# Cross attention over 16 batches: another beginning, input copies in four parts, value sums in pairs of steps, values in three pieces

## The reference

```python
x = x + xattn(layernorm(x), ctx_1024, ctx_1024, Wq, bq, Wk, bk, Wv, bv, Wo, bo)
x = x + attn_ref(layernorm(x), ...)     # Mamba block and MLP
x = x + ffn_ref(layernorm(x), ...)      # 8 experts, 2 chosen per token

def xattn(query, key, value, ...):      # D 128, 16 heads of 8, batches 16, queries 64, keys 1601
    q = split_heads(query @ Wq.T + bq)
    k = split_heads(key @ Wk.T + bk)
    v = split_heads(value @ Wv.T + bv)
    scores = einsum('bhqd,bhkd->bhqk', q, k) / sqrt(8)
    weights = softmax(scores, axis=-1)
    out = einsum('bhqk,bhkd->bhqd', weights, v)
    return out.transpose(0, 2, 1, 3).reshape(b, -1, 128) @ Wo.T + bo
```

## Time and profile before

| what | us |
|---|---|
| median of 3 runs (range) | 650.39 (646.67 to 653.92) |
| the profiled execution | 646.16 |
| its span in the trace | 644.3 |
| start to the first scores of batch 0 | 67.6 |
| the 16 rounds of attention | 67.6 to 422 |
| Mamba, MLP and experts | 422 to 644.3 |

### The profile page before, as it was taken

One profiled execution on the slowest core, in us unless ns is written; L12 is line 12 of the kernel. 1 busy time (PEld: TensorE's weight loads), 2 busy tenths in 40 slices (PEclk: granted clock), 3 DMA queues, 4 the chain that ended last, 5 costly groups with the idle time before them and its releaser, 6 DMA issues. The chain is left out here.

```text
span 644.3 us, 17592 instructions
## 1 busy us (share of the span) xinstructions
PE 544.0 (84%) x7470; PEld 356.4 (55%) x7470; DVE 442.6 (69%) x755; ACT 353.7 (55%) x641; POOL 254.6 (40%) x138
## 2 busy tenths in 40 slices
PE   2666899898897898999999989855677888999997
PEld 1232555554564554555565556542356566777776
DVE  5365878776785776888788878069887575454544
ACT  4641477666675576677677768932742423333331
POOL 3184676646645654657566310078045000000000
PEclk9985799998998999999999999995858779999999
DMA  5736764753753835844763250023002000000001
GB/s 178 113 99 99 100 155 87 131 69 65 132 67 65 133 43 90 131 59 93 114 80 57 39 68 4 3 68 88 1 5 107 1 1 2 1 0 0 1 0 34
DMA packets 16117, 41.56 MB, mean 65 GB/s; under 512 B 3190, under 2 KB 6014, under 8 KB 15930
## 3 DMA queue, kind: packets, MB, share of 16 engines
q1 hardware_dynamic: 15324, 40.09, 34.8%
q10 hardware_dynamic: 720, 0.41, 0.2%
HBM read 19.70 MB, written 0.52 MB: 31 GB/s over the span
## 5 line engine op out<-in xcount | busy, mean ns | idle before, releaser
L603 DVE TENSOR_REDUCE half_max<-wide 128x2 f32<-128x802 f32 x256 | 243.6, 989 | 69.1 <-PE wide L376 64.7
L527 ACT ACTIVATE probs<-score 128x512 f32<-128x512 f32 (+1 forms) x416 | 225.5, 594 | 64.6 <-PE score L396 64.2
L413 PE MATMUL sums<-probs,values 128*32 128x192 f32 (+3 forms) x3328 | 135.9, 282 | 9.7 <-issue 8.0
L413 PEld LDWEIGHTS sums<-probs,values 128*32 128x32 f32 (+1 forms) x3328 | 88.2, 110 | 66.9 <-issue 33.2
L376 PE MATMUL wide<-k_stack,q_cur 48*128 48x401 bf16 x512 | 91.3, 354 | 8.5 <-DVE half_max L603 4.0
L396 PE MATMUL score<-q_cur,k_stack 50*128 50x128 bf16 (+1 forms) x1664 | 85.1, 222 | 13.0 <-issue 5.5
L396 PEld LDWEIGHTS score<-q_cur,k_stack 50*128 50x128 bf16 (+1 forms) x1664 | 51.4, 96 | 43.2 <-issue 15.2
L289 POOL TENSOR_TENSOR ctx_hi<-ctx_in,one 128x1601 bf16<-128x1601 f32 x15 | 42.9, 2859 | 74.4 <-PE wide L327 67.6
L1549 DVE SCALAR_TENSOR_TENSOR hid_e<-gu,keep_bgu,gate 114x512 f32<-114x512 f32 x48 | 35.9, 750 | 52.0 <-ACT gate L1464 52.0
L1464 ACT ACTIVATE gate<-gu,gate_bias 114x512 f32<-114x512 f32 x48 | 32.9, 687 | 68.3 <-PE gu L1430 65.1
L298 POOL TENSOR_TENSOR k_hi<-k_full,one 128x1601 bf16<-128x1601 f32 x15 | 42.9, 2857 | 69.1 <-ACT k_full L496 69.1
(11 more groups left out here) (230 smaller groups left out, 722.6 us busy)
## 6 DMA issues: line engine op xcount, KB each, us to landing
k_stack<-k_hi SPq DMA_DIRECT2D x64, 204.0 KB, 6.0
ctx_in<-in_ctx SPq DMA_DIRECT2D x15, 800.5 KB, 10.8
k_stack<-k_lo SPq DMA_DIRECT2D x32, 204.0 KB, 9.0
w_stage<-in_wgu SPq DMA_DIRECT2D x8, 342.0 KB, 3.0
keep_w<-in_w SPq DMA_DIRECT2D x1, 1368.0 KB
keep_x<-in_x SPq DMA_DIRECT2D x1, 512.0 KB, 6.8
q_cur<-shift SPq DMA_DIRECT2D x32, 2.0 KB
out<-keep_x SPq DMA_DIRECT2D x2, 256.0 KB, 2.5
```

Source lines behind the costliest of these rows:

```text
L413: last = pe.matmul(sums[32 * g:32 * g + 32, first * LQ:(first + heads) * LQ], values[0:m, n, k, VW * g + 2 * c:VW * g + 2 * c + 32], probs ...
L527: nc.scalar.activation(probs[0:m, step % NPROB, :].rearrange("r (g p c) -> r p g c", g=G, p=2)[:, p], score[0:m, (2 * step + p) % NSCORE, ...
L603: dve.tensor_reduce(half_max[:, b % 2, :, u // 4, u % 4], wide[:, w, :].rearrange("p (c k) -> p c k", c=2)[:, :, 0:CH], AX.X, ALU.max).the ...
```

## The change

**Beginning.** Rounds -2 and -1 are gone. TensorE now runs, in this order: keys 0, the turned inputs and the queries (first those of tokens 0 to 127 alone, in one item of four 128-column products; 5 query items where there were 4), values 0, keys 1, the 16 units of batch 0 with the two halves of keys 2 after units 7 and 10, the turn, values 1. GpSimd's first split waits until the layer norm's last small operation on VectorE is done. ScalarE takes the first keys before and between the layer norm's operations.

**Rounds.** `units_at` starts batch 1 at step 0 of round 0, two units a step, and batch 2 at step 10 of round 0 (in 11 steps); from batch 3 on nothing changes. Step 0 sums steps 10 and 11 of the round before, step 1 sums step 12, steps 3, 5, 7, 9, 11 sum two steps each; the even steps sum nothing. Values go in three pieces (5, 4, 4 blocks) in steps 2, 4 and 6, keys in steps 8 and 10 (9 and 11 in round 0).

**Copies.** From round 1 on, SP waits on the score counter between the pieces: first pair of `k_hi` copies at once, the second after step 0's scores, `k_lo` after step 2's, and the context as four copies of 32 partitions, one each after the scores of steps 4, 5, 6 and 7.

```diff
-V_STEPS, K_STEPS = (1, 4), (6, 8)
+V_STEPS, K_STEPS = (2, 4, 6), (8, 10)
+V_BLOCKS = (0, 5, 9, NK)
+H_STEP, L_STEP, C_STEP = 1, 3, 5
+K2_UNITS = (7, 10)
...
 def units_at(i, k):
-    return [(b, u) for b in (i + 1, i + 2) if 0 <= b < B for u in range(16)
-            if NK * (b - 1) - LEAD + NK * u // 16 == NK * i + k]
+    found = []
+    for b in (i + 1, i + 2):
+        lead = {1: 0, 2: 3}.get(b, LEAD)
+        found += [(b, u) for u in range(16) if 1 <= b < B and
+                  NK * (b - 1) - lead + (lead + 8) * u // 16 == NK * i + k]
+    return found
+def keys_at(i, k):
+    steps = K_STEPS if i else (9, 11)
+    return [(i + PREFETCH, steps.index(k))] if k in steps and i + PREFETCH < B else []
...
+            def at_step(i, k):
+                if i >= 1:
+                    sp.wait_ge(s_score, 2 * (NK * i + k))
...
-                sp.dma_start(ctx_in[:, b % 2, :], A["ctx"][:, b, :]).then_inc(s_ctx[b % 2], 16)
+                for r in range(4):
+                    at_step(i, C_STEP + r)
+                    rows = slice(32 * r, 32 * r + 32)
+                    sp.dma_start(ctx_in[rows, b % 2, :], A["ctx"][rows, b, :]).then_inc(s_ctx[b % 2], 16)
...
                 for t in range(2):
+                    if t:
+                        at_step(i, H_STEP)
                     for half in HALVES:
                         at = half + PAIR * t
                         sp.dma_start(k_stack[at:at + PAIR, n, :, :], k_hi[half:half + 64, :]).then_inc(done, 16)
+                at_step(i, L_STEP)
...
+            pool.wait_ge(s_norm, 1)
             split(1)
...
-            for i in range(-2, B):
+            for i in range(B):
                 for k in range(NK):
-                    if i >= 0:
-                        scores(i, k)
+                    scores(i, k)
                     units = units_at(i, k)
                     if units:
                         maxima(*units[0])
                     if i >= 1 and k == 0:
+                        sum_values(i - 1, NK - 3)
+                        sum_values(i - 1, NK - 2)
+                    if i >= 1 and k == 1:
                         sum_values(i - 1, NK - 1)
-                    if i >= 0 and k == 2:
-                        sum_values(i, 0)
-                    if i >= 0 and k >= 2:
-                        sum_values(i, k - 1)
+                    if k >= 3 and k % 2:
+                        sum_values(i, k - 3)
+                        sum_values(i, k - 2)
                     for unit in units[1:]:
                         maxima(*unit)
                     if k in V_STEPS and i + 2 < B:
                         vals(i + 2, V_STEPS.index(k))
-                    if k == turn_step(i) and 0 <= i + 1 < B:
+                    if k == turn_step(i) and i + 1 < B:
                         turn_max(i + 1)
-                    if k in K_STEPS and i + PREFETCH < B:
-                        keys(i + PREFETCH, K_STEPS.index(k))
+                    for half in keys_at(i, k):
+                        keys(*half)
```

More of the change, by code:

```diff
@@ L327, in product3, with turn_x, queries @@
                 return pe.matmul(out, lhs_lo, rhs_hi, start=False, stop=True)
[L329 to L334, removed]
-                last.then_inc(s_wide, 1)
[L337 to L343, removed]
+            def turn_x(part):
+                w, first = half_free(pe, ("x", part, 0)), TOKENS[part]
+                for t in range(first // P, TOKENS[part + 1] // P):
+                    pe.wait_ge(s_xn, t + 1)
+                    last = pe.transpose(wide[:, w, t * P - first:t * P - first + P], xn[:, t, :], keep.ident[:])
+                last.then_inc(s_wide, 1)
+            def queries(part, pair):
+                w, toks = half_free(pe, ("q", part, pair)), slice(TOKENS[part], TOKENS[part + 1])
+                is_empty(pe, ("x", part, 0))
+                for j in range(2 if part else G):
+                    at = 512 * j if part else P * j
+                    last = pe.matmul(wide[:, w, at:at + toks.stop - toks.start], wq[:, 2 * pair + j, :],
+                                     xnT[:, toks], start=True, stop=True)
                 last.then_inc(s_wide, 1)
@@ L356, in keys, with vals @@
                 last.then_inc(s_wide, 1)
[L358 to L361, removed]
+            def vals(b, part):
+                n, w, first = b % 2, half_free(pe, ("v", b, part)), V_BLOCKS[part]
+                for k in range(first, V_BLOCKS[part + 1]):
+                    at = P * (k - first)
                     ks = slice(k * P, k * P + P)
@@ L424, in _ @@
             turn_x(0)
+            queries(0, 0)
             turn_x(1)
[L426 to L430, removed]
+            turn_x(2)
+            for _, part, pair in Q_ORDER[1:]:
+                queries(part, pair)
+            for part in range(3):
+                vals(0, part)
+            for half in range(2):
+                keys(1, half)
+            for u in range(16):
+                maxima(0, u)
+                if u in K2_UNITS:
+                    keys(2, K2_UNITS.index(u))
+            turn_max(0)
+            for part in range(3):
+                vals(1, part)
+            for i in range(B):
                 for k in range(NK):
-                    if i >= 0:
-                        scores(i, k)
+                    scores(i, k)
                     units = units_at(i, k)
@@ L461, in _, with first_keys @@
                 nc.scalar.copy(ctx_hi[:, 0, ks], ctx_in[:, 0, ks]).then_inc(s_first, 1)
[L462 to L470, removed]
+            def first_keys(half):
                 w = filled(act, ("k", 0, half))
@@ L498, in keys_out, with first_vals_out @@
                     bias=keep.vecs[:, V_BK:V_BK + 1]).then_inc(s_by_act, 1)
[L500 to L505 removed]
+            def first_vals_out(b, part):
+                w, first = filled(act, ("v", b, part)), V_BLOCKS[part]
+                for k in range(first, V_BLOCKS[part + 1]):
+                    at = P * (k - first)
+                    last = nc.scalar.copy(
+                        values[:, b % NSLOT, k, :].rearrange("p (g c) -> p g c", g=G)[:, :, 1:VW - 1],
+                        wide[:, w, at:at + P].rearrange("p (g c) -> p g c", g=G))
                 last.then_inc(s_by_act, 1)
@@ L531, in _ @@
-                    if i >= 1 and k == 0:
+                    for p in range(2):
+                        act.wait_ge(s_score, 2 * step + p + 1)
+                        if p == 0 and step >= NPROB:
+                            act.wait_ge(s_pv, step - NPROB + 1)
+                        nc.scalar.activation(
+                            probs[0:m, step % NPROB, :].rearrange("r (g p c) -> r p g c", g=G, p=2)[:, p],
+                            score[0:m, (2 * step + p) % NSCORE, :].rearrange("r (g c) -> r g c", g=G), ACT.Exp,
+                            scale=HD ** -0.5).then_inc(s_exp, 1)
@@ L532, in _ @@
+                    if i >= 1 and k == 1:
                         sums_out(i - 1)
[L533 to L536 removed]
+                    for half in keys_at(i, k):
+                        keys_out(*half)
             sums_out(B - 1)
@@ L626, in shifts @@
                 dve.sem_inc(s_by_dve, 1)
-            for i in range(-2, B):
+            for u in range(16):
+                maximum(0, u)
+            row_maxima(0)
+            shifts(0)
+            for i in range(B):
                 for k in range(NK):
```

163 lines of the change are left out of this document (93 added, 70 removed).

## The result

The changed kernel takes 663.70 us (median of 4 runs, 661.55 to 666.64), the kernel before 649.58 (4 runs, 646.67 to 653.92). The ratio is 1.0215, with a 95% interval of 1.014 to 1.029: slower by some 2%. The forecast was 654 with 629 to 668: the time lies in the range, 10 us above the point. The profiled execution took 662.41 us (span 660.6), 16.25 more than the profiled one of before.

The account below looks back on a forecast made before the run. TensorE, near full, was taken to bound quiet rounds, with late instructions and half clock adding some 20 us, and the keys' way hidden. Sum: -3 + 12 x (24.2 - 23.2) - 1 = +8 on 646.16, 654 us; range 629 to 668.

Parts of the forecast that it names:

- Keys two steps later: Keys in steps 8 and 10: the loop becomes the longest limit, 24.2 us a round (23.2 to 25.3), where it was 23.2.
- M + 23.7: Earliest start of the next batch's first unit, M being this batch's first unit: 5.2 to second keys, 18.5 to the stack.
- the loop: Way from a batch's first unit through second keys, GpSimd split and k_stack copies to the next batch's first unit; 20.0 us before.
- Spread copies: k_stack copies go out as before, context leaves the burst; worth 0 to 1.7 us a round, taken as 0.
- Take 0 on top of the loop: Taking the context out of the burst of copies adds no gain, since the longer loop covers it.
- Nothing binds at the waits: SP's waits on step 0's and step 2's scores delay no k_stack copy: GpSimd gives k_hi and k_lo later anyway.
- Pairs of sums: Rounds: pairs save TensorE 0.7 us but bare VectorE waits grow from 2.0 to 2.7; quiet round 21.8 us (20.8 to 22.5).
- Beginning: Start to batch 3's maxima: first maxima near 32.5, first scores 57.6, batch 3's maxima 101.5; -3 us (0 to -6).
- End: Last rounds: round 13 has no keys, 14 and 15 are ScalarE's; -1 us (0 to -2.5).
- Quiet and short: Rival: loop under 22 us, instructions no longer late, 625 us; decided by keys to stack under 16.5 us; chance 0.20.
- Slower: Rival: loop binds without covering instruction stalls, which delay the keys; 25.6 us a round, 671 us; chance 0.15.
- Does nothing: Rival: pairs and spread bring nothing, the loop stays hidden; 642 us; chance 0.10.

## Why the prediction was right, and where it was off

**The deciding step held.** "Keys two steps later" forecast a loop of 5.2 + 18.5, with TensorE standing before each first maximum and a clock loss in half of the rounds, 24.2 us. Measured: 5.14 in seven of twelve loops, 6.6 to 7.6 in the five with a stretch at half clock (the window at 325.00 is one), 17.8 to 18.4 to the stack, 24.12 in all. That it met 24.2 so closely is in part luck: a loop at full clock is 23.4, where M + 23.7 was said, and half clock adds 1.9 us on average in five of twelve, where 1.1 in half of them was said. (By the text's own numbers the upper bound is 23.7 + 1.1 = 24.8, not 25.3, and the sums at the bounds are 642 and 667, not 643 and 670.) Keys alone moved in the kernel before cost 22 us, and moved back in the changed kernel they give 23. TensorE stands before the maxima for 1.1 us on average in the eleven waits, where I said 2.

**Spread copies.** "Take 0 on top of the loop" held within 4 us. "Nothing binds at the waits" held for the changed kernel (k_lo at 240.56, GpSimd done at 240.5; k_lo goes out 3.3 us after the first k_hi with the waits and without). What the text did not see is that it depends on the keys' steps: with keys in 6 and 8 the wait on step 2's scores does hold k_lo, by 1.6 us, and that alone gives 19 us. The upper bound, 1.7 us a round or 20 in all, was about right for the kernel before (20 measured); I credited it to the context copy, and that part gives 5 to 8.

The Trainium skill's Runtime: NRT & Kernel Launch, Instruction fetch mechanics, says that crossing a block is mostly hidden. By it the stalls would have stayed when copies were moved; they fell from 13.8 to 2.6 us when two copies were held back by 1.6 us. The measurement decides: among six copies of 204 KB it isn't hidden in every round here. What the Trainium skill's DMA: Bandwidth & Descriptors, Rules for kernel authors, says against parts by partitions agrees with the runs: 640.6 in four parts, 643.2 whole and late, no clear difference.

**Pairs of sums.** A quiet round without the loop was forecast at 21.8, between 20.8 and 22.5; it is 22.3 in both kernels that show it. The waits rise by more than the 0.7 us a round that I had: with keys in 6 and 8 those for VectorE and ScalarE are 22.0 + 12.2 us in some 12 rounds, before 6.0 + 3.0, so 2.1 us more in each; 0.8 of it is ScalarE's, which I hadn't counted. Less work on TensorE gives a part back.

**Beginning, the first term that failed.** -3 was forecast, between 0 and -6; it is +2.6 in the profiled pair and about -0.6 by the means. The 3.4 us by which the profiled execution of before lies under its median, which the text put down to late instructions, are for the most part this: its batch 3's maxima stand 3.3 us before the mean of the seven. The forecast step failed either way: first maxima at 32.5, where no trace has them before 36.1. Of the 6 us by which batch 3's maxima are late against 101.5, 4.7 are there. By the text's own sum (36.2 - 32.5, and 4 put back) all that ends with the queries was to be over some 7.7 us earlier. The queries do start earlier, but run at half clock until 25.4 and then one item at a time, and are over 0.5 us earlier in the pair (2.6 by the means). From first maxima to first scores it is 25.4 us (25.1 forecast), from there to batch 3's maxima 45.0 (43.9).

**End, the second.** -1 was forecast and +2.7 measured. Rounds 14 and 15 were called ScalarE's, rightly, but a pair of sums holds the next scores for longer than two exponentials last. 1.02 us is in the earlier trace rows and the exponentials' length is in the profile; the text didn't set them beside each other for rounds without maxima.

The sum was +8 and is +16 in the profiled pair (+14 by the medians): the mechanism right, the loop off by -1, both ends together by some 9 us in the pair, or 6 with the beginning taken by its means.

**Rivals.** "Quiet and short" asked for less than 16.5 us from keys to stack: it is nowhere under 17.5. "Slower" came in its mechanism where the copies aren't spread (25.0 a round with late keys alone) and not here. "Does nothing" fell with the waits at 0.09 us.

## What to carry to other kernels

Before moving a producer, add up the whole way from the consumer that releases it, through every engine and copy, to the consumer's next turn; where that comes near the length of a round, a move is free only up to the slack (1.4 us here), and what goes beyond it is added to every round. Work put in pairs saves switches on its own engine and takes away the cover of the others: set the pair's length beside what the neighbour has left to do, in each kind of round. And when an engine stands without a reason in the profile, look at what DMA was queued when its next instruction block came: holding the last two of six copies back by 1.6 us gave 3% here.

## What the runs showed that I had not expected

- **A gap of some 2 us within a burst of copies lets instruction blocks come sooner, and costs the copies nothing.** Six k_stack copies land 12.4 to 13.6 us after the first issue however k_lo is held back, and the blocks that went with stalls, 7.7 to 14.0 us after that issue before, start 1.8 to 5.2 us sooner in five of seven places. TensorE's stalls fell from 13.8 to 2.6 us and the mean granted clock rose from 0.915 to 0.929.
- **Half clock follows the stalls.** From 78 to 415 it was granted in six stretches of 3.4 us in the kernel before, five of them from 125 to 230, and in one with the waits alone. The gain of 19 us is more than the 11 us of stalls that went. It doesn't follow each stall: with keys in 7 and 9 there are five of 1.05 to 2.4 us in the rounds and no half clock from 73 to 437.
- **A TensorE wait for a DMA can be labelled issue**, as before the maxima of the changed kernel; landing times tell the two apart.
